# One pooling step fewer ahead of the paired stretch, and GpSimd's third low transfer ahead of x's second combination

## What is computed

```python
# x: (16, 512, 512); layer 0: a two-layer MLP whose last 128 outputs use weights of one of 16 experts
h = gelu(x @ fc1_w.T + fc1_b)                       # 512 -> 2048, exact gelu
shared = h @ fc2_w.T + fc2_b                        # 2048 -> 384
expert = h @ experts_w[indices].T + experts_b[indices]   # 2048 -> 128
x = x + concatenate([shared, expert])
# layer 1: additive attention pooling over the 512 tokens with one of three masks for each batch
scores = tanh(x @ W1 + b1) @ v
mask = (l <= j, l >= j or l != j)[prompt_type]      # prefix, postfix, all but oneself
pooled = softmax(where(mask, scores, -1e30)) @ x / count(mask)
x = x + pooled
```

## Time and profile before

| | |
|---|---|
| median of 3 runs | 1424.59 us (1422.02 to 1425.33) |
| the profiled execution | 1422.57 us, span 1420.8 us |
| mean granted TensorE clock | 0.976 |
| ScalarE, VectorE, GpSimd busy | 68%, 75%, 18% of the span |
| paired batches | 12, one each 88 us or so |

### The profile page before, as it was taken

How to read it: one execution, slowest core, us unless ns; L and a number is a source line. 1 busy time by engine, 2 the same in 40 slices (tenths; PEclk the granted TensorE clock), 3 DMA queues, 4 the chain that set the end, 5 groups by cost and what they waited for, 6 DMA issues and landing times.

```text
span 1420.8 us, 25573 instructions
## 1 busy us (share of the span) xinstructions
PE 1329.3 (94%) x9849; PEld 976.8 (69%) x9849; DVE 1069.5 (75%) x2092; ACT 966.8 (68%) x1764; POOL 260.2 (18%) x380
## 2 busy tenths in 40 slices
PE   9999999998979999899897989979999899898998
PEld 5457484766858677686775857758677686776855
DVE  7888897767678685876858758587585875858788
ACT  5769678584856858578585775857748578485772
POOL 0000101212222121221212212122121221212301
PEclk9999999999999999999999999999999999999999
DMA  7530223235353353533425335253352533525206
GB/s 278 176 99 16 45 82 68 67 93 116 83 114 75 98 109 83 119 83 96 105 77 119 83 95 106 75 119 83 89 110 77 120 82 90 110 77 119 69 18 119
DMA packets 73885, 136.43 MB, mean 96 GB/s; under 512 B 9747, under 2 KB 34211, under 8 KB 71331
## 3 DMA queue, kind: packets, MB, share of 16 engines
q0 software_dynamic: 28032, 56.63, 23.2%
q1 hardware_dynamic: 45154, 77.38, 16.3%
q10 hardware_dynamic: 576, 0.79, 0.2%
HBM read 45.65 MB, written 18.87 MB: 45 GB/s over the span
## 4 chain that ended last, share of the span: by engine, by line
PE 67%; DVE 12%; ACT 9%; DMA 6%; issue 3%; POOL 1%; POOLq 0%; DVEq 0%; SPq 0%
PE ps L547 12%; PE ps L549 12%; PE ps L548 12%; PE ps L660 5%; DMA hl<-hl 5%; PE ps L657 4%; PE ps L636 4%; PE ps L637 4%; PE ps L638 4%; ACT g L1033 2%; ACT ee L1007 2%; ACT hh L1007 2%; DVE ee L1621 1%; DMA g<-space 1%; DVE space L2085 1%
## 5 line engine op out<-in xcount | busy, mean ns | idle before, releaser
L547 PE MATMUL ps<-xh,w1h 128*128 128x256 f16 x960 | 261.7, 273 | 0.0
L548 PE MATMUL ps<-xl,w1h 128*128 128x256 f16 x960 | 261.7, 273 | 0.0
L549 PE MATMUL ps<-xh,w1l 128*128 128x256 f16 x960 | 261.7, 273 | 0.0
L1033 ACT ACTIVATE g<-ps,b1s,ds 128x512 f32<-128x512 f32 x240 | 173.5, 773 | 65.4 <-PE ps L549 65.4
L547 PE MATMUL ps<-xh,ch 128*128 128x256 f16 x720 | 196.3, 273 | 0.0
L549 PE MATMUL ps<-xh,cl 128*128 128x256 f16 x720 | 196.2, 273 | 0.0
L548 PE MATMUL ps<-xl,ch 128*128 128x256 f16 x720 | 196.2, 273 | 0.0
L1621 DVE SCALAR_TENSOR_TENSOR hl<-g,ix,hh 128x512 f16<-128x512 f32 x243 | 177.0, 745 | 3.1
L1007 ACT ACTIVATE hh<-g,ix 128x512 f16<-128x512 f32 x243 | 161.5, 718 | 0.0
L1007 ACT ACTIVATE ps<-ps 128x256 f32<-128x256 f32 x192 | 71.2, 371 | 119.1 <-PE ps L660 80.4
L2668 POOL DMA_DIRECT2D g<-space x30 | 36.9, 1230 | 628.9 <-DMA g<-space 570.3
(11 more groups left out here) (364 smaller groups left out, 3192.4 us busy)
## 6 DMA issues: line engine op xcount, KB each, us to landing
space<-in_xT SPq DMA_DIRECT2D x62, 256.0 KB, 3.1
g<-space SPq DMA_DIRECT2D x60, 256.0 KB, 2.6
er<-in_ew SPq DMA_DIRECT2D x15, 1024.0 KB, 4.9
out<-space SPq DMA_DIRECT2D x60, 256.0 KB, 2.4
space<-space POOLq DMA_DIRECT2D x52, 256.0 KB, 3.3
hl<-hl POOLq DMA_DIRECT2D x24, 512.0 KB, 7.6
g<-space POOLq DMA_DIRECT2D x30, 256.0 KB, 4.5
g<-g POOLq DMA_DIRECT2D x30, 256.0 KB, 4.1
```

Of the source, the lines that this page charges most:

```text
L547: mm(to, wh, mh, start=i in (1, 5) and c == 0, stop=False, skip_group_check=True)
L548: mm(to, wh, ml, start=False, stop=False, skip_group_check=True)
L549: m = mm(to, wl, mh, start=False, stop=c == 1, skip_group_check=True)
L1033: act(in_two(g_of(b, k)), src, ACT.Gelu, bias=b1s[:, k:k + 1], scale=ds1[:, b % 2, p:p + 1]).then_inc(gelu_done)
```

## The change

In batch 3 the first cycle takes two pooling steps ahead of `add_second` in place of three. All later counts stay, so from there on every place holds the step before the one that it held; in the last batch `late` has one more, behind the first two expert lows, so that the total is the same. Of a batch's pooling, ten steps instead of eleven then stand ahead of the paired stretch: step 11 goes from behind the last `add_second` to the `pool(2)` behind `expert_sum2`. And in GpSimd's `sum_quarters` the third sum's low transfer goes ahead of the combination T1.

```diff
             elif b == 3:
-                takes = ((0, 3, 1), (1, 1, 1), (1, 2, 1), (1, 1, 1), (1, 1, 1), (1, 1, 1))
+                takes = ((0, 2, 1), (1, 1, 1), (1, 2, 1), (1, 1, 1), (1, 1, 1), (1, 1, 1))
             elif b == LAST:
-                takes, late = ((0, 1, 1), (1, 1, 1), (1, 1, 1), (0, 0, 0), (0, 0, 0), (1, 0, 0)), (1, 1, 0, 1)
+                takes, late = ((0, 1, 1), (1, 1, 1), (1, 1, 1), (0, 0, 0), (0, 0, 0), (1, 0, 0)), (1, 1, 0, 2)
...
             add_quarters(b, T3, quarter(b, 0, 1))
-            add_quarters(b, T1, quarter(b, 0, 0))
             if paired(b - 1):
                 third_low_sum(b - 1)
+            add_quarters(b, T1, quarter(b, 0, 0))
             if b > 2:
                 fetch(b - 2)
```

## The result

The changed kernel takes 1305.7 us (median) beside 1424.12 for the kernel before on the same chip: a ratio of 0.917, 95% interval 0.915 to 0.919. Its profiled execution has a span of 1304.0 us, 116.8 less than before. It was forecast at 1306, in the range of 1298 to 1348, with a chance of 0.92 for faster. One of the four executions of the changed kernel took 7808.98 us, at a granted clock of 1.0, for a reason that the record doesn't show; the other three took 1305.45 to 1305.8, and the ratio rests on them.

What follows compares the result with a forecast made beforehand. TensorE bounds the kernel, idling in 12 correction stretches because VectorE is late behind step 11's wait. Each falls from 35.09 to 25.2 us, 12 x 9.9 = 119; 1422.57 becomes 1303.7, plus 2.0 gives 1306 us, range 1298 to 1348.

Steps and rivals of the forecast that it cites:

- the 12 stretches: TensorE, last `main` matmul to next batch's first product, once per paired batch: 35.09 us to become 25.2, 119 in all.
- Step 11 leaves the lows: VectorE: step 11 behind the expert sums waits for no exponentials; hl 15 comes at about 745.8 instead of 752.2.
- The slow clock: TensorE behind its second wait: first 8 matmuls take 1.89 us against 1.05 later; wait and slow clock were to go.
- The low transfer: GpSimd's third-sum transfer, issued before T1: starts 746.4, takes some 4.6 us, lands 751.0, wanted 754.6, 3.6 us to spare.
- The rule on VectorE and GpSimd's transfers: VectorE operations taking both shared ports stop GpSimd writing DMA descriptors; by it the low transfer would land at 752.8.
- The kept 0.5 us: TensorE at correction 5 in each stretch: a 0.5 us wait for the first sum, against 2.7 in all before.
- the thinnest margin: Fourth sums' transfers: last lands at 767.3, TensorE wants it at 767.4 or 767.9; 0.1 to 0.6 us to spare.
- 24.7: One stretch without waits at full clock, in us: 28 blocks of 0.87 = 24.4, last `main` matmul 0.2, small sum 0.1.
- The first rival: GpSimd's ring serializes transfers, TensorE stands 3.5 us per batch, 42 in all: 1348 us; chance 0.22 including a late engine.
- the sign that the prediction named for this rival: A stretch of 28 or 29 us with TensorE waiting for a fourth-sums transfer, or for ScalarE's first copy.
- The second rival: Step 11's wait on VectorE only moves and just GpSimd's order acts: 59 us gained, 1366 us; chance 0.08.
- The slower rival: Late exponentials block VectorE's third, second and first sums; worse than before past 758.2, 1446 us at 760; chance 0.05.

Runs made afterwards that it cites:

- the last experiment: Changed kernel with SP's put into the place of h's tile 14, and tile 15's behind it, held until the low transfer landed: 1309.84 us, ratio 0.921.

## Why the prediction was right, point by point

- **Where the time was.** Only the 12 stretches changed; their sum fell by 116.8 us where 119 was worked out, and the span by the same.
- **How exact the number was** is in part luck. The stretches came out 1.8 us longer in sum than forecast (304.24 against 12 x 25.2), and the profiled execution took 1305.8 where 1303.7 was worked out. The forecast then added 2.0 us, because the median before lay that much above the profiled execution; after the change it does not (1305.7 and 1305.8). The two cancel, and so 1306 meets 1305.7.
- **Step 11 leaves the lows.** Times of the followed batch, forecast (less 47.7) and measured: `hl` 15 at 698.1 and 698.1; step 11 without a wait; end of exponentials 698.5 and 698.5; start of the second sum of hh 705.6 (the 753.3 at which correction 1 ends) and 705.69; start of the first sum 716.7 and 716.55. Counting each row of VectorE behind the last event that it really needs gave all of them within 0.2 us. That the wait is the cause, and not the number of steps, is shown by the two kernels that move the exponentials and the two that move one more step.
- **The slow clock.** The 1.89 us for eight matmuls behind the second wait are 1.04 now, at a granted clock of 1.00, as assumed.
- **The low transfer** was mis-sized: 4.6 us assumed, 6.2 measured, since SP's puts move their data ahead of it. I had taken the ee transfer as the like case without asking what SP starts with the same `low`. It was free because the sum had 3.6 us to spare for it; 2 were left.
- **The rule on VectorE and GpSimd's transfers** was left open by the rows of before. Here the low transfer is issued at 698.58 (698.47 with the puts held back), beside two 16-bit sums of VectorE that end at 700.5, and with the puts away it lands after 4.8 us, against 4.6 for the ee transfer: held by nearly 2 us it was not. I had also read the rule too widely. The Trainium skill, page "SBUF — State Buffer", section "Who interferes with whom", says that a `tensor_tensor` has no mode that takes both ports and, with both inputs in SBUF, contends only with GpSimd's reads; that this leaves the writing of descriptors alone, it marks as inferred. The expert sums are TENSOR_TENSOR rows, and the run agrees. The wide reading stands both in the prediction and in theory 2 of the last experiment. That two transfers in one time share the same 16 engines, and come one behind the other, is what the page's section "Can I just issue two DMAs to hit both halves?" states; the 6.2 us against 4.8 agree with it.
- **The kept 0.5 us** for the first sum measured 0.35 in most stretches; but the fourth sums' last transfer, which I had as the thinnest margin (0.1 to 0.6 us), was late by 1.5 and 1.7 in the last two. The two errors have opposite signs: 24.7 + 0.35 = 25.05 in the eight typical stretches, 25.35 in the mean, 25.2 forecast. In these two the transfer took 10.8 and 10.6 us where it took 8.7 in the followed batch:

```profile
hl<-hl POOLq DMA_DIRECT2D x1, 512.0 KB, 10.6
```

  Why is open. In the kernel with ee's own semaphore the same two batches have it again (10.5 and 10.4 us), so it is no accident of one execution. A fetch of instructions falls into the end of both transfers in the changed kernel, which is a coincidence in time; nothing was tried on it.
- **The first rival** (transfers serialize) had its mechanism half right. T1 did wait until T3 had landed, but low transfer and T3, and the three fourth sums, are issued back to back; the forecast's 42 us did not come. A transfer that is held by an earlier one makes TensorE wait only in the kernel with late puts. The last two stretches of the changed kernel show the sign that the prediction named for this rival, TensorE waiting for the fourth sums, but not its mechanism: there too the three are issued back to back and on time (the first 7.8 us into the stretch, as in the followed batch).
- **The second rival** (GpSimd's part alone) was priced at 1366 and the kernel that is just this took 1383: I took the whole 44.4 us as gone and did not ask what is late next there, the first sum.
- **The slower rival** was rightly placed, with one correction. Its mechanism costs exactly what it says once it bites (2.94 us late, 2.9 us paid), but it begins to take back gain as soon as the exponentials end after step 11's start, 1.9 us behind where they do end. From step 11 to the end of the hl sum it is 7.6 us (700.43 to 708.05), and 7.5 by the prediction's own times, where the rival was priced with 7.1.

## What to carry to other kernels

Where an in-order engine stands for something that the work behind it does not need, move that one instruction behind the urgent work rather than making anything faster: a 0.75 us step in the wrong place cost 103 us here (78 with GpSimd's new order), and one step more or less cost about its own length or less. Price a pair of edits on one chain together, for their gains overlap (103 and 38 alone, 118 together), and for each removed wait ask what is late next. When several transfers add to one semaphore, look whether each waiter needs all of them; and when a transfer must be quick, list what the same event, or one just ahead of it, releases on the other queues.

## What the hardware showed that I had not expected

- An accumulating transfer of 512 KB that lands 4.8 us behind its issue when SP's two puts are held back took 6.2 us when they were issued 0.5 and 1.1 us ahead of it: the puts moved 0.44 MB in 1.3 us at a full share of all 16 DMA engines before its data moved.
- The two levels of TensorE's clock (1.2 and 2.4 GHz) made a wait of 2.1 us cost 3.8. The length of the wait alone does not decide it. Behind 1.5 and 1.7 us in the changed kernel the granted clock stayed at 1.00; behind 1.68 us it fell in one stretch with the step alone, while with the exponentials late it fell in two stretches and stayed at 1.00 in ten with waits like it. With GpSimd's order alone it stayed at 1.00 in a stretch with waits of 2.61, 0.77 and 1.73 us. Before, the 3.7 us ahead of 765.44 cost another 0.9 in the first eight matmuls alone. What decides is open.
- In these rows GpSimd starts a transfer that has its inputs either about 0.55 us behind the last one or only when an earlier one has landed. In the changed kernel ee, hh and hl (512 KB each) are issued 0.54 us apart; with T2's combination (256 KB) issued late, the third of them was issued 1.6 us later than in the changed kernel. That its queue holds only so much fits this; no limit was measured.
